# The second layer's experts in pairs: 128 inner rows each and two times 48 inner rows together

## The reference, cut to what matters

```
x = x + tanh(g_ffn[1]) * L1_ffn(layernorm(x))
scores = softmax(x @ gate_w);  topk_w, topk_idx = top_k(scores, 2)          # 8 experts, 2 chosen per token
g      = silu(x @ w_gate[e]) * (x @ w_up[e])                                # w_gate, w_up: 256 x 176
routed = sum over the 2 chosen e of  comb[e] * (g @ w_down[e])              # w_down: 176 x 256
shared = (silu(x @ sw_gate) * (x @ sw_up)) @ sw_down                        # 256 x 352
out    = routed + shared
```

## Time and profile before

| | |
|---|---|
| median of 3 runs | 1172.62 us (1172.27 to 1174.23) |
| span of the profiled execution | 1171.5 us |
| TensorE busy | 1066.6 us (91%) |
| routed experts of the second layer, first hidden product to last | 1050.7 to 1144.7 us |
| rounds of one block there | 2.49 us |

### The profile page before, as it was taken

How to read it: one execution, slowest core, us unless ns; L and a number is a source line. 1 busy time by engine, 2 the same in 40 slices (tenths; PEclk the granted TensorE clock), 3 DMA queues, 4 the chain that set the end, 5 groups by cost and what they waited for, 6 DMA issues and landing times.

```text
span 1171.5 us, 24138 instructions
## 1 busy us (share of the span) xinstructions
PE 1066.6 (91%) x8396; PEld 608.8 (52%) x8396; DVE 956.1 (82%) x1748; ACT 892.2 (76%) x1546; POOL 702.5 (60%) x626
## 2 busy tenths in 40 slices
PE   8988898889988988898889988999999999999995
PEld 5743444444444444444444447756654455557774
DVE  6999999999999999999999996853328888843335
ACT  4779999999999999999999996635534567734440
POOL 3016888888787878787878785457641001543331
PEclk9999999999999999999999999799999999999998
DMA  6797987888788888888776664867937003433326
GB/s 192 121 163 146 171 171 162 171 171 173 161 171 171 173 164 173 173 169 164 155 118 110 112 109 65 244 182 213 316 98 300 1 0 85 138 102 101 102 89 222
DMA packets 388928, 176.36 MB, mean 151 GB/s; under 512 B 330542, under 2 KB 373779, under 8 KB 388809
## 3 DMA queue, kind: packets, MB, share of 16 engines
q1 hardware_dynamic: 382104, 157.85, 62.2%
q0 software_dynamic: 6480, 16.77, 4.2%
q10 hardware_dynamic: 224, 0.20, 0.1%
HBM read 52.70 MB, written 43.59 MB: 82 GB/s over the span
## 4 chain that ended last, share of the span: by engine, by line
PE 51%; DVE 33%; ACT 5%; issue 5%; DMA 3%; POOL 2%; SPq 1%; POOLq 0%; ACTq 0%; DVEq 0%
DVE top L426 26%; PE bank L234 10%; PE bank L220 9%; PE bank L1187 4%; PE bank L2599 4%; PE bank L252 4%; PE bank L1580 3%; PE bank L2615 3%; PE bank L1174 2%; PE bank L1166 2%; ACT weight L485 2%; PE bank L270 1%; PE bank L1598 1%; PE bank L682 1%; POOL dispatched_rows L1823 1%
## 5 line engine op out<-in xcount | busy, mean ns | idle before, releaser
L485 ACT ACTIVATE weight<-bank,bias,sq_all 128x1024 uint8<-128x1024 f32 x512 | 610.2, 1201 | 24.1 <-PE bank L234 18.9
L426 DVE TENSOR_REDUCE top<-bank 128x1 f32<-128x512 f32 (+1 forms) x683 | 610.1, 951 | 11.9 <-PE bank L220 1.6
L537 POOL CAST weight<-turned 128x2048 bf16<-128x2048 uint8 x256 | 479.4, 1895 | 44.8 <-PE bank L252 23.2
L234 PE MATMUL bank<-kT,query 128*128 128x512 bf16 x1024 | 307.7, 382 | 11.8 <-ACT weight L485 4.8
L252 PEld LDWEIGHTS bank<-v_sb,weight 128*128 128x128 bf16 x4096 | 172.0, 97 | 103.4 <-POOL weight L537 1.9
L220 PE MATMUL bank<-kT,qspace 64*128 64x512 bf16 x687 | 134.9, 386 | 55.0 <-DVE top L426 55.0
L252 PE MATMUL bank<-v_sb,weight 128*128 128x16 bf16 x4096 | 172.5, 170 | 0.6 <-POOL weight L537 0.6
L220 PE MATMUL bank<-kT,query 128*128 128x512 bf16 x337 | 127.8, 379 | 1.6 <-DVE top L426 1.4
L234 PEld LDWEIGHTS bank<-kT,query 128*128 128x128 bf16 x1024 | 59.8, 96 | 103.8 <-ACT weight L485 61.8
L1823 POOL DMA_INDIRECT dispatched_rows<-qspace,put x32 | 37.1, 1161 | 117.8 <-DVE qspace L2376 108.6
L485 ACT ACTIVATION_READ_ACCUMULATOR weight<-bank,bias,sq_all 128x1 f32 x512 | 101.3, 198 | 0.0
(11 more groups left out here) (350 smaller groups left out, 1466.2 us busy)
## 6 DMA issues: line engine op xcount, KB each, us to landing
dispatched_rows<-zeros SPq DMA_DIRECT2D x32, 524.0 KB, 3.2
answered_rows<-zeros SPq DMA_DIRECT2D x16, 512.0 KB, 3.2
late<-answered_rows SPq DMA_DIRECT2D x16, 512.0 KB, 6.3
erow<-dispatched_rows SPq DMA_DIRECT2D x39, 131.0 KB, 2.1
wgu<-in_L_ffn_w_gate SPq DMA_DIRECT2D x26, 176.0 KB, 3.9
wgu<-in_L_ffn_w_up SPq DMA_DIRECT2D x26, 176.0 KB, 3.9
query<-qspace SPq DMA_DIRECT2D x32, 128.0 KB, 3.1
turned<-weight SPq DMA_TRANSPOSE x256, 3.1
```

Source lines behind the costliest of these rows:

```text
L234: mm = pe.matmul(unit[u % 2][:, v * 512:(v + 1) * 512], query2[:, t % 2, h, :], kT[:, h // 2, first + v * 512:first + (v + 1) * 512], star ...
L426: ve.tensor_reduce(top[:, first:first + count], bank[:, first % 3:first % 3 + count, :], AX.X, ALU.max).then_inc(s_max, 1)
L485: ac.activation(weight8[:, n % BYTES, u * 1024:(u + 1) * 1024], unit[u], ACT.Exp, bias=bias[:, n:n + 1], scale=sq_all[:, n:n + 1], accum_o ...
L537: po.tensor_copy(weight[:, n % 3, :, :, :].rearrange("p c q two -> p (c q two)"), turned8[:, n % 3, :, :].rearrange("p c q -> p (c q)").bi ...
```

## The change

The second layer's routed experts get the form of the first layer's. Blocks 2j and 2j+1 are a pair (20 of them, NPAIR1; the last has one block). `eh1` holds 128 columns of the even block, 64 of both remainders (48 and 16 zeros each, set once by a memset), 128 of the odd one. `turn_hidden(j)` makes three transposes; `copy_hidden(j)` copies 384 columns; `answer(j)` makes two products over 128 inner rows, then one over partitions 0 to 47 and one over partitions 64 to 111, into PSUM banks 6 and 7. `multiply` becomes two instructions (128 and 48 columns).

A block's expert is known only at run time. The 48 rows that an even block needs lie on partitions 0 to 47 for all 8 experts, loaded with the others. Those of an odd block must lie on partitions 64 to 111: they are fetched for each pair by SP (`fetch_rest(j)`, a register read of `owner_u` and a transfer of 48 rows) into a ring of 7 (RESTS). The first 7 are issued between the wait for the tables and the first `fetch_rows`; the others, from j = 7 to 18, behind `fetch_rows(2j-3)`, waiting for `answer(j-7)`. TensorE waits for the fetch between the two 48-row products. Rows are still turned one block ahead.

```diff
-                w1d = sw[0:FC, 0:E1 * 2 * C].rearrange("p (e c n) -> p e c n", e=E1, c=2)
+                w1d = sw[:, 0:E1 * C].rearrange("p (e n) -> p e n", e=E1)
+                w1d_rest = sw[:, E1 * C:2 * E1 * C].rearrange("p (e n) -> p e n", e=E1)
...
-                            sp.dma_start(w1d[:, e, :, :], a["L1_ffn_w_down"][e].rearrange("(c p) n -> p c n", p=FC)).then_inc(s_w1, 16)
+                            sp.dma_start(w1d[:, e, :], a["L1_ffn_w_down"][e, 0:P, :]).then_inc(s_w1, 16)
+                        sp.dma_start(w1d_rest[rest_rows(0), :, :], a["L1_ffn_w_down"][:, P:F1, :].rearrange("e p n -> p e n")).then_inc(s_w1, 16)
...
+                        def fetch_rest(j):
+                            if j >= RESTS:
+                                sp.wait_ge(sx_["answers"], E0 + 2 * (j - RESTS) + 2)
+                            e = sp.value_load(owner_u[0:1, 2 * j + 1:2 * j + 2], min_val=0, max_val=E1 - 1)
+                            sp.dma_start(w1d_rest[rest_rows(1), j % RESTS, :], a["L1_ffn_w_down"][e, P:F1, :]).then_inc(rest_loaded(j)[0], 16)
+
                         sp.wait_ge(mx_["tables_ready"], 1)
+                        for j in range(RESTS):
+                            fetch_rest(j)
                         sp.wait_ge(mx_["mixed_ready"], NG)
                         sp.wait_ge(mx_["mixed_turned"], NG)
                         sp.wait_ge(s_scatter1, 16 * NT * K1)
                         for b in range(NB1):
                             fetch_rows(b)
+                            if b % 2 == 1 and RESTS <= (b + 3) // 2 < NB1 // 2:
+                                fetch_rest((b + 3) // 2)
...
+                        def turn_hidden(j):
+                            both = len(pair_blocks(j))
+                            pe.wait_ge(sx_["hidden"], E0 + 2 * j + both)
+                            if j >= 2:
+                                pe.wait_ge(sx_["hidden_copied"], E0 // 2 + j - 1)
+                            for k in range(both + 1):
+                                mm = pe.transpose(bank[:, 4 + j % 2, k * P:(k + 1) * P], eh1[:, j % 2, k * P:(k + 1) * P], ident[:])
                             mm.then_inc(sx_["hidden_turned"], 1)
...
+                        def answer(j):
+                            pe.wait_ge(sx_["hidden_copied"], E0 // 2 + j + 1)
+                            for i, b in enumerate(pair_blocks(j)):
+                                if b >= 2:
+                                    pe.wait_ge(sx_["answers_weighted"], E0 + b - 1)
+                                pe.matmul(bank[:, 6 + i, 0:C], ehT1[:, j % 2, 2 * i, :], w1d[:, expert[b], :], start=True, stop=False)
+                            for i, b in enumerate(pair_blocks(j)):
+                                if i == 1:
+                                    pe.wait_ge(*rest_loaded(j))
+                                pe.matmul(bank[:, 6 + i, 0:C], ehT1[rest_rows(i), j % 2, 1, :],
+                                          w1d_rest[rest_rows(i), expert[b] if i == 0 else j % RESTS, :], start=False, stop=True).then_inc(sx_["answers"], 1)
+                                expert.pop(b)
...
-                        for b in range(NB1 + 2):
-                            if b + 1 < NB1:
-                                load_owner(b + 1)
-                                turn_rows(b + 1)
-                            if b < NB1:
+                        for j in range(NPAIR1 + 2):
+                            for b in pair_blocks(j) if j < NPAIR1 else ():
+                                if b + 1 < NB1:
+                                    load_owner(b + 1)
+                                    turn_rows(b + 1)
                                 hidden(b)
-                            if 0 <= b - 1 < NB1:
-                                turn_hidden(b - 1)
-                            if b >= 2:
-                                answer(b - 2)
+                            if 0 <= j - 1 < NPAIR1:
+                                turn_hidden(j - 1)
+                            if j >= 2:
+                                answer(j - 2)
...
-                            if b >= 2:
-                                weigh(b - 2)
+                            for b in pair_blocks(j - 2) if j >= 2 else ():
+                                weigh(b)
```

More of the change, by code:

```diff
@@ L2540, in program @@
                     erow1, erowT1 = se("erow1", [P, RING1, ROW1]), se("erowT1", [P, 2, CK, P])
-                    esil1, eh1, ehT1 = se("esil1", [P, 2, F1]), se("eh1", [P, 2, F1]), se("ehT1", [FC, 2, 2, P])
+                    NPAIR1 = (NB1 + 1) // 2
+                    esil1, eh1, ehT1 = se("esil1", [P, 2, F1]), se("eh1", [P, 2, 3 * P]), se("ehT1", [P, 2, 3, P])
                     yrow1 = se("yrow1", [P, YRING, C])
@@ L2551, in got1_group, with rest_loaded, pair_blocks @@
                         return (got_early if g < 2 else got_late)[:, (g % 2) * G:(g % 2 + 1) * G, k * C:(k + 1) * C]
+                    RESTS = SLOTS - RING1
+                    def rest_loaded(j):
+                        s = RING1 + j % RESTS
+                        return s_ew[s], weights_loaded(s, len(range(s, E0, SLOTS))) + 16 * (j // RESTS + 1)
+                    def pair_blocks(j):
+                        return range(2 * j, min(2 * j + 2, NB1))
                     def last_answers(g, k):
@@ L2600, in hidden @@
                             mm.then_inc(sx_["hidden_products"], 1)
-                        def turn_hidden(b):
-                            pe.wait_ge(sx_["hidden"], E0 + b + 1)
-                            if b >= 2:
-                                pe.wait_ge(sx_["hidden_copied"], E0 // 2 + b - 1)
-                            for c in range(2):
-                                mm = pe.transpose(bank[0:FC, 4 + b % 2, c * P:(c + 1) * P], eh1[:, b % 2, c * FC:(c + 1) * FC], ident[:])
-                            mm.then_inc(sx_["hidden_turned"], 1)
@@ L2610, in answer @@
-                        def answer(b):
-                            pe.wait_ge(sx_["hidden_copied"], E0 // 2 + b + 1)
-                            if b >= 2:
[L2613 to L2617, removed]
+                        def turn_hidden(j):
[5 more added lines that the diff above has]
+                                mm = pe.transpose(bank[:, 4 + j % 2, k * P:(k + 1) * P], eh1[:, j % 2, k * P:(k + 1) * P], ident[:])
+                            mm.then_inc(sx_["hidden_turned"], 1)
@@ L2619, in experts1_tensor @@
                         expert = {}
-                        pe.wait_ge(s_w1, 16 * 3 * E1)
+                        pe.wait_ge(s_w1, 16 * (3 * E1 + 1))
                         pe.wait_ge(mx_["tables_ready"], 1)
@@ L2625, in experts1_tensor @@
                         turn_rows(0)
-                        for b in range(NB1 + 2):
-                            if b + 1 < NB1:
-                                load_owner(b + 1)
-                                turn_rows(b + 1)
-                            if b < NB1:
+                        for j in range(NPAIR1 + 2):
[3 more added lines that the diff above has]
+                                    turn_rows(b + 1)
                                 hidden(b)
-                            if 0 <= b - 1 < NB1:
-                                turn_hidden(b - 1)
-                            if b >= 2:
-                                answer(b - 2)
+                            if 0 <= j - 1 < NPAIR1:
+                                turn_hidden(j - 1)
+                            if j >= 2:
+                                answer(j - 2)
                         pe.wait_ge(sx_["rows_scaled"], E0 + NB1)
                         pe.wait_ge(sx_["hidden"], E0 + NB1)
-                        pe.wait_ge(sx_["hidden_copied"], E0 // 2 + NB1)
+                        pe.wait_ge(sx_["hidden_copied"], E0 // 2 + NPAIR1)
                         for g in (NG - 2, NG - 1):
@@ L2668, in experts1_scalar @@
                         copy_rows(0)
[L2669 to L2672, removed]
+                        for j in range(NPAIR1 + 2):
+                            for b in pair_blocks(j) if j < NPAIR1 else ():
+                                if b + 1 < NB1:
+                                    copy_rows(b + 1)
                                 silu(b)
-                            if b >= 2:
-                                weigh(b - 2)
+                            for b in pair_blocks(j - 2) if j >= 2 else ():
+                                weigh(b)
                     def experts1_vector(ve):
@@ L2694, in multiply @@
                             ve.wait_ge(sx_["silu"], E0 + b + 1)
[L2695 to L2703, removed]
@@ L2705, in experts1_vector @@
-                        for b in range(NB1 + 1):
-                            if b < NB1:
+                            j = b // 2
+                            if j >= 2:
+                                ve.wait_ge(sx_["hidden_turned"], E0 // 2 + j - 1)
+                            main, rest = 2 * P * (b % 2), P + KB * (b % 2)
```

(21 more changed lines are left out.)

## The result

| | before | after |
|---|---|---|
| median | 1172.68 us (17 runs) | 1174.3 us (17 runs) |
| ratio of the runs | | 1.0014 (95% interval 1.0007 to 1.002) |
| span of the profiled execution | 1171.5 us | 1172.1 us |

The change makes the kernel slower, by 1.6 us or 0.14%. That is less than the 0.2% that I had called measurable, but 17 runs on each side tell it from nothing. Forecast were 0.8 us less.

The account below looks back on a forecast made before the run. TensorE's work was taken to bound the steady stretch, GpSimd's scatters the end. Of 3.8 us gained, 1.4 went in the tail and 1.6 in front: 0.8 us less, 1171.8 us; range 1169.3 to 1176.4.

Parts of the forecast that it names:

- SP in front: Start of the stage: seven fetches on SP's queue take 8.3 us and delay the first rows, and TensorE, by 1.6 us.
- Rival 4: Start of the stage: reads as slow as the longest seen make the front cost 1.5 us more, 1173.3 us; chance 0.08.
- The bounds, 1.5 to 3.1: Start of the stage: delay in us from seven fetches if register reads are the shortest or the longest seen.
- TensorE's steady work: Steady stretch: a pair takes 4.78 us for 4.98 in two old rounds; 19 pairs gain 3.8 us.
- rival 2: TensorE's answers: the 48-row products don't overlap, 0.87 us for 0.63, costing 4.6 us, 1176.4 us; chance 0.14.
- ScalarE's margin: Steady stretch: the hidden-rows copy behind two weighings is ready 0.13 us before TensorE needs it, so no cost booked.
- Rival 1: Steady stretch: ScalarE's copy comes late, each 0.1 us past the margin costing 1.8 us; 1175 us and up; chance 0.12.
- The tail: After the last hidden product starts: TensorE through at 7.1 us, last scatter at 9.59; scatters set the end; 1.4 us lost.
- Rival 3: Start of the stage: the seven fetches cost nothing, 1170.2 us, or 1169.3 with a smaller tail loss; chance 0.20.

Follow-up runs that it names:

- e1_warm: The change with seven extra 256-column products keeping TensorE at work in the idle time before the first rows; median 1172.81 us, 1.0002 of before.
- e1_four: The change with four fetches of 48 weight rows ahead of the first row fetch instead of seven; median 1170.9 us, repeated 1170.64 us.
- e2_six: The change with six fetches of 48 weight rows ahead of the first row fetch instead of seven; median 1173.04 us, 0.9997 of before.
- e1_before_front: The kernel before, with seven unused register reads and 48-row transfers added ahead of its first row fetch; median 1176.53 us, 1.0031 of before.
- e1_late: The change with all 19 fetches of 48 weight rows behind row fetches, none in front; median 1171.23 us, 0.9993 of before.

## Why the prediction was wrong

**The step that failed** is the one headed "SP in front": "Delay 1.6 us, and it goes whole to TensorE, which has nothing else to do". The delay was there; what it does to TensorE was not thought through. I counted the idle time and not what comes after it. From the first hidden product to the third there are 4.26 us after (1052.31 to 1056.57) and 2.81 with four in front (1050.55 to 1053.36): the halved clock costs 1.45 us, to which some 0.2 for the second transposes come. `e1_warm` gives 1.5 by the medians. No rival named the clock, and the forecast's sum had no term for it. Rival 4 (the front costs more, 1173.3) comes nearest to the time, but its reason, slow reads, is only 0.3 us of it.

**The delay itself was too small in the sum.** Forecast 1.6; the rows leave SP 2.15 us later (2.75 behind the event for 0.60), and the first hidden product starts 2.27 later (6.41 less 4.14), 0.2 of it those transposes. The seven fetches took 8.6 us for 8.3 (1039.29 to 1047.91), and the tables were ready 0.35 us later against the common event than in the execution that I read (6.99 ahead of it before, 6.64 after). The bounds, 1.5 to 3.1, held.

**TensorE's steady work was right.** Pairs of 4.79 for 4.78; from the first hidden product to the last it took 88.5 us, for 87.0 forecast plus the 1.45 of the clock. The 48-row products overlap in spite of the wait and the register operations between them (0.63), so rival 2 is ruled out; the transposes behind them take 0.37 for 0.22, the forecast 0.15 more.

**ScalarE's margin held.** In the change a copy behind two weighings ends at 1098.91 (1098.54 + 0.37), and the weights of the product that needs it begin to load at 1099.29:

```profile
1097.82 0.84 ACT L2692 ACTIVATE yrow<-bank,summed 128x256 f32<-128x256 f32 x2 [1.50 <-PE bank L2642]
1098.54 0.37 ACT L2679 COPY erowT<-bank 128x256 f32<-128x256 f32 x1
...
1099.29 0.89 PEld L2621 LDWEIGHTS bank<-late,erowT 128*128 128x128 f32 x4
```

That is 0.38 us less the 0.15 for the way between the engines, 0.23 for the forecast 0.13. Rival 1 did not come about: the waits view of TensorE has two waits for ScalarE in the whole stage, 1.1 us together, and both are in the tail.

**The tail was half right.** The scatters behave as forecast: five in a row at 1.28, the last at 9.73 us behind the last hidden product, for 9.59. TensorE's end was mis-sized: 7.78 for 7.1 (and 7.1 is itself 0.1 above its own terms, 6.12 + 0.87). Two waits for ScalarE were in the sum, but the answers behind them began 0.3 and 0.4 us later than I took (4.03 and 6.53 for 3.74 and 6.12), and the last block's answer takes 1.25 for 0.87: 0.63 from the start of its full product to its 48-row product, and 0.62 from there to the shared answers. With that the later chain is TensorE's and not the scatters', which I had as the one that sets the end. In `e1_four` it is the scatters' again, VectorE waiting 0.96 us for the fetched answers.

**The sum after the fact**, from the profiled executions: 3.8 us gained in the steady stretch; 2.3 lost by the delay and 1.45 by the clock; 1.55 lost in TensorE's tail (96.26 us from the first hidden product to the last shared answers, less 1.45 of clock, are 94.8, only 2.25 under the 97.05 of before); and 0.2 back, as VectorE no longer waits for the fetched answers. 3.8 - 2.3 - 1.45 - 1.55 + 0.2 = -1.3, the loss seen from the common event. Set against the forecast, TensorE's last shared answers were to start 1.3 us earlier and start 1.5 later: 0.7 more of delay, 1.45 of clock that was put at nothing, and 0.7 more of tail. The clock is the largest of the three. Without it the change is level with before, as `e1_warm` is (1172.81), and still 1.0 above the forecast.

**Rival 3**, the front at no cost, was put at 1170.2 us. The change did not meet it, since seven fetches take 8.6 us; with four of them the front does cost nothing, and that kernel comes near the rival's time: 1170.9 and 1170.64.

What stays open: the tail. That TensorE loses about 1.5 us there is read from the trace; the one attempt to win it back only moved the wait.

## What to carry to other kernels

When something is put ahead of a chain that TensorE waits for, the price is the delay and also the clock that the longer idle time costs: here 2.3 us of delay drew another 1.5 behind it. Prefetches belong in the slack that the queue has, counted in items: SP had room for four here and six were too many (five was not tried); with all of them behind the first rows TensorE waited for rows, 0.7 us by the profile, though the medians do not tell that kernel from four in front. And when a change reorders a pipeline into larger units, work out its last units one by one, with each bank that must be emptied: 1.5 of 3.8 us were lost there, and the forecast of TensorE's end had 0.9 of them.

## What the runs showed that I had not expected

TensorE's clock fell behind an idle time of 2.02 us in `e2_six`, of 2.97 in `e1_before_front` and of 3.10 in the change, but not behind 0.96 us in `e1_late` or 0.93 in the kernel before. In each of these a second, shorter wait follows (0.59, 0.74, 0.53, 0.53 and 0.64 us), so what is shown is the fall behind such a pair of waits and not behind the longer one by itself. Before them the engine had been at work at full clock (7.00 of 7.00 us from 1040 to 1047 in the change). The clock did not fall at once: the transposes that follow the longer idle time ran at full speed (0.41 us for two), and the next ones, about 1 us later, were slower (0.69; 0.57 in `e1_before_front`). It came back while TensorE worked without a gap: the third hidden product of the change, at 1056.57, takes 1.35 us again.
